# Two graph-attention layers on one core: the first output projection tile by tile with the normalization in it, and a head end in two parts

## The reference

```python
x1 = relu(x @ W_ah + b_ah)
xs = [relu(gat_conv(x1, src, dst, W, a_s, a_d, b)) for W, a_s, a_d, b in three]   # 4 heads of 192 each
y  = relu(concatenate(xs, axis=1) @ W_out + b_out)        # [1250, 2304] @ [2304, 768]
x2 = layernorm(x + y)
h  = elu(gat_layer(x2, W1 [768, 2048], 4 heads of 512) + b1)
z  = gat_layer(h, W2 [2048, 768], 1 head) + b2
return layernorm(x2 + z)
```

## Time and profile before

| | us |
|---|---|
| median of 3 runs | 2097.6 (2096.47 to 2100.13) |
| the profiled execution | 2099.49 |
| its span (first to last instruction) | 2097.7 |
| PE busy | 1865.0 (89%) |
| DVE busy | 1492.5 (71%) |
| ACT busy | 974.5 (46%) |

### The profile page before, as it was taken

How to read it: one execution, slowest core, us unless ns; L and a number is a source line. 1 busy time by engine, 2 the same in 40 slices (tenths; PEclk the granted TensorE clock), 3 DMA queues, 4 the chain that set the end, 5 groups by cost and what they waited for, 6 DMA issues and landing times. The chain is left out here.

```text
span 2097.7 us, 29944 instructions
## 1 busy us (share of the span) xinstructions
PE 1865.0 (89%) x11272; PEld 1774.4 (85%) x11272; DVE 1492.5 (71%) x2490; ACT 974.5 (46%) x1463; POOL 166.1 (8%) x139
## 2 busy tenths in 40 slices
PE   5998899994999999994989889979999996999888
PEld 4666689994999999994989779978999995999888
DVE  7887759996888888862556619717888885235776
ACT  1222222215687897763222322217888885232433
POOL 5010022100000000000001012100000000000210
PEclk9999999996999999996999889989999998999999
DMA  3111154335243424307856445544423404644402
GB/s 115 49 53 49 38 157 147 104 87 137 65 130 95 108 87 123 89 13 219 236 138 184 137 149 151 169 129 131 143 82 106 139 34 132 176 108 131 116 1 74
DMA packets 203354, 237.69 MB, mean 113 GB/s; under 512 B 98741, under 2 KB 177677, under 8 KB 203224
## 3 DMA queue, kind: packets, MB, share of 16 engines
q1 hardware_dynamic: 195240, 208.32, 34.5%
q0 software_dynamic: 7216, 24.91, 4.0%
q10 hardware_dynamic: 768, 2.70, 0.4%
HBM read 173.99 MB, written 61.90 MB: 112 GB/s over the span
## 5 line engine op out<-in xcount | busy, mean ns | idle before, releaser
L946 PE MATMUL p_o<-h_in,p 125*125 125x193 f32 x2400 | 405.5, 332 | 41.5 <-DVE p L905 20.9
L946 PEld LDWEIGHTS p_o<-h_in,p 125*125 125x125 f32 x2400 | 399.3, 191 | 44.8 <-issue 23.7
L866 ACT ACTIVATE e<-uv,col 125x1250 f32<-125x1250 f32 x240 | 298.5, 1358 | 16.0 <-DMA uv<-uv_rows 14.9
L1404 PE MATMUL p_o<-p_hi,h_parts 125*128 125x416 f32 (+1 forms) x960 | 282.8, 355 | 24.7 <-DVE p_lo L1338 18.4
L1686 PE MATMUL p_y<-fw_hi,f_hi 128*125 128x384 f32 (+1 forms) x680 | 237.9, 350 | 60.7 <-DVE f_lo L1562 58.6
L1686 PE MATMUL p_y<-fw_lo,f_hi 128*125 128x384 f32 (+1 forms) x680 | 235.3, 346 | 0.0
L1686 PE MATMUL p_y<-fw_hi,f_lo 128*125 128x384 f32 (+1 forms) x680 | 234.6, 345 | 0.0
L1562 DVE TENSOR_TENSOR f_lo<-f_raw,f_hi 128x1125 fp32r<-128x1125 f32 (+1 forms) x80 | 101.1, 1265 | 173.6 <-ACT f_hi L1660 173.5
L900 DVE TENSOR_TENSOR e<-e 125x1250 f32<-125x1250 f32 x120 | 174.1, 1451 | 67.5 <-ACT e L866 67.4
L1404 PEld LDWEIGHTS p_o<-p_hi,h_parts 125*128 125x128 f32 x960 | 181.7, 189 | 30.8 <-issue 18.6
L1660 ACT ACTIVATE f_hi<-f_raw 128x1125 fp32r<-128x1125 f32 (+1 forms) x80 | 87.4, 1093 | 251.3 <-PE p_y L1686 215.3
(11 more groups left out here) (227 smaller groups left out, 3259.4 us busy)
## 6 DMA issues: line engine op xcount, KB each, us to landing
f_raw<-turned SPq DMA_DIRECT2D x40, 562.5 KB, 4.3
f_raw<-turned SPq DMA_DIRECT2D x40, 500.0 KB
h_rows<-h_out SPq DMA_DIRECT2D x32, 560.0 KB
h_parts<-h_rows SPq DMA_DIRECT2D x40, 448.0 KB
uv<-uv_rows SPq DMA_DIRECT2D x24, 546.9 KB
turned<-out_f SPq DMA_DIRECT2D x18, 625.0 KB
h_rows<-h_out SPq DMA_DIRECT2D x24, 424.4 KB
h_in<-h_rows SPq DMA_DIRECT2D x24, 424.4 KB
```

The costliest lines, as they stand in the source:

```text
L866: last = a.activation(e[:, g % RING, kind, :], uv[:, hh, kind, :], ACT.Exp, bias=col_src[kind][:, bass.ds(i * 2 + hh, 1), s])
L946: last = nc.tensor.matmul(p_o[:, b, n * 256:n * 256 + C0 + 1], p[:, g % RING, d * T:(d + 1) * T], h_in[:, hh, s, 0:C0 + 1], start=(s == 0 ...
L1404: last = nc.tensor.matmul(p_o[:, bank(n, c), 0:w], h[:, s, kind, cols].bitcast(F32R), pp[:, g % RING, 0:w], start=(s == 0 and j == 0), sto ...
```

## The change

1. `aggregate_layer0`: `divisors` works in two parts. The first takes the sums of tiles 0 to 3 (banks 0 and 1) as soon as PE has finished tile 3 in the head's last step (`banks_done`), the second those of tiles 4 to 9 at the step's end. ACT waits for the first part ahead of tile 0 and for the second ahead of tile 4. DVE stands one step earlier for it (after g = 11 and g = 1 in place of 12 and 2).
2. `turned0` is laid out `[NT, 128, KO, T]`: a store writes runs of 500 bytes, and a piece of a tile is read in runs of 4,500 bytes.
3. `G` is stored to memory (3.1 MB) behind the loads of the second iteration. After the last load of the stage, its place takes the first five of 18 blocks of `w_out`, all 768 columns each, and the first piece of tile 0.
4. `project_out_layer0` takes the place of `from_turned` and `normalize`: all of `w_out` stays on chip as two roundings, the tiles are done once, both halves of the columns in two PSUM banks, and each tile is normalized when it is summed, with tiny instructions of one column, and stored to `x2_rows`. `x` is loaded into three slots.
5. `project_layer1` loads the rows of `x2` in four slots, turns five tiles ahead of the first product and the other five between the first tiles, adds `b2` on DVE and stores the sum to `base_rows`; the scores come after tile 9, the mask is loaded back, and the maxima begin at tile 18.
6. `aggregate_last` loads `base_rows`; POOL's additions are gone.

```diff
@@ aggregate_layer0
             load(0)
             load(1)
+            dma_in_two(sp, core.mask_rows, core.G.rearrange("p t n -> p (t n)"), mask_saved)
...
+            for k in range(W_AHEAD):
+                sp.dma_start(w_ahead[:, k, :], w_out[:, k * 128:(k + 1) * 128, :].rearrange("h p c -> p h c")).then_inc(ahead_in, 16)
+            sp.dma_start(f_ahead[:, 0], turned_rows[0, :, 0:KO // 2, :]).then_inc(ahead_in, 16)
             store(ITERS - 2)
             store(ITERS - 1)
...
+                        if s == NT - 1 and d == 2 * FIRST - 1:
+                            last.then_inc(banks_done, 1)
@@ project_out_layer0 (new), DVE
+            for t in range(1, NT):
+                rest_of_f(t, 0)
+                for n in range(weighed.chunks * (t - 1) // (NT - 1), weighed.chunks * t // (NT - 1)):
+                    weighed.reduce(dve, n, ...)
+                rest_of_f(t, 1)
+                leave(t - 1)
+            leave(NT - 1)
@@ project_layer1, SP
+            load_x(0)
+            load_w(0)
+            dma_in_two(sp, b_row[:], bias.rearrange("(o f) -> o f", o=1).broadcast_to([T, D]), bias_in)
+            for t in range(1, XR):
+                load_x(t)
+            load_w(1)
+            for t in range(XR, NT):
+                store_base(t - XR)
+                load_x(t)
@@ aggregate_last
-        @block.gpsimd
-        def _(pool):
-            pool.wait_ge(base_in, 64)
-            for t in range(NT):
-                pool.tensor_tensor(y2[:, t, :], y2[:, t, :], b_row[:], ALU.add).then_inc(base_done, 1)
```

More of the change, by code:

```diff
@@ L887, in divisors @@
             def divisors(i, hh):
[L888 to L893, removed]
+                for n, (b0, b1) in enumerate(((0, FIRST), (FIRST, BANKS))):
+                    if n == 0:
+                        dve.wait_ge(banks_done, i * 2 + hh + 1)
+                    else:
+                        dve.wait_ge(p_used, i * STEPS + ((hh + 1) * NT + 2 * NT))
+                    v.tensor_scalar(sums[:, 0, 2 * b0:2 * b1].rearrange("p (b n) -> p b n", n=2),
+                                    p_o[:, b0:b1, :].rearrange("p b (n c) -> p b n c", n=2)[:, :, :, C0],
+                                    1e-16, None, ALU.add).then_inc(sum_steps, 1)
+                    dve.wait_ge(sum_steps, (i * 2 + hh) * 4 + 2 * n + 1)
+                    v.reciprocal(sums[:, 1, 2 * b0:2 * b1], sums[:, 0, 2 * b0:2 * b1]).then_inc(sum_steps, 1)
             def body(i, first):
@@ L986, in project_layer1 @@
         p_h = pb("p_h", [T, 4, 512])
-        p_r = pb("p_r", [R, 3, 512])
+        p_r = pb("p_r", [128, 3, 512])
         p_s = pb("p_s", [128, 512])
+        bias_in = sem("bias_in")
+        mask_in = sem("mask_in")
+        x_loaded = [sem(f"x2_loaded{r}") for r in range(XR)]
+        x_turned = sem("x2_turned")
+        x_rounded = sem("x2_rounded")
+        x_split = sem("x2_split")
+        base_done = sem("base_done")
+        base_stored = [sem(f"base_stored{r}") for r in range(XR)]
         w_in = [sem(f"pw_in{u}") for u in range(2)]
@@ L1038, in _ @@
                 sp.wait_ge(h_stored[part], 64 * UNITS)
+            for r in range(XR):
+                sp.wait_ge(base_stored[r], 32 * len(range(r, NT, XR)))
             sp.wait_ge(uv_stored, 32)
@@ L1077, in _ @@
                     act.wait_ge(uv_turned, 1)
[L1078 removed]
+                    a.activation(turned_uv[:], p_s[0:heads * NT, 0:2 * T].rearrange("p (a q) -> p a q", a=2), ACT.Copy).then_inc(uv_kept, 1)
                     act.wait_ge(uv_kept, 1)
@@ L1112, in spread @@
                 v.scalar_tensor_tensor(v_col[:, 0:heads, :], score[:, 1], SLOPE, tmp2[:], ALU.mult, ALU.subtract).then_inc(max_steps, 1)
+            for t in range(TURNED_FIRST):
+                rest_of_x(t)
             for n in range(TILES):
                 q, t = divmod(n, NT)
+                if n + TURNED_FIRST < NT:
+                    rest_of_x(n + TURNED_FIRST)
+                if n == NT:
+                    keep_scores()
                 dve.wait_ge(h_rounded, n + 1)
@@ L1148, in _ @@
                 last.then_inc(h_summed, 1)
+                if n + TURNED_FIRST < NT:
+                    turn_x(n + TURNED_FIRST)
+                if n == NT - 1:
+                    scores()
+                    turn_scores()
                 if n == UV_AT + 4:
@@ L1796, in aggregate_last @@
-def aggregate_last(nc, core, h2, uv, col_src, bias, x2_dram, y2, out):
+def aggregate_last(nc, core, h2, uv, col_src, base_rows, y2, out):
     CT = core.CT
```

432 lines of the change are left out of this document (293 added, 139 removed).

## The result

The changed kernel takes 2063.27 us (median of 4 runs, 2061.53 to 2063.97), the kernel before 2098.86 beside it (2096.47 to 2100.46): a ratio of 0.9832, 95% interval 0.9815 to 0.9848. The gain is 35.6 us; 46.6 was forecast (2097.6 to 2051). The profiled execution's span is 2061.2 us against 2097.7, 36.5 less. Cut at landmarks that both traces have, these 36.5 lie as follows.

A forecast was written before the change was run, and what follows sets the result against it. PE, 89% busy, was taken to bound the kernel, so its idle time was counted: -16.5 - 0.2 - 29.5 + 5.8 - 5.9 = -46.3 us against the median 2097.6 gave 2051. Its own range was 2042 to 2060, the wider one 2036 to 2069.

The forecast's parts named there:

- rival 1: After the projection, x2's round trips set PE's pace: cycle of 6 us, first product at 22, 2068 us; 15 in 100.
- Heads, -16.5: Ends of heads in the first aggregation: of 20.7 us of PE's idle time some 4 stay; bounds -20.7 and -11.
- The last head's stores, +1.1: End of the first aggregation: stores in 500-byte runs cost +1.1 us, from 0 to +4; with fewer copies, -0.2 together.
- the rate of reads of 500-byte runs: Last head's stores: 6.50 MB read in some 20 us, 325 GB/s, so 0.64 MB of stores take 2.0 us.
- The doubling that it noted: Last head's stores: by the skill's 512-byte rule the last store takes about twice as long, the sum some 2 us more.
- Projection, 196.8: First projection, load to last sum: tile 0 in 28.4 us, tiles 1 to 9 in 168.4; against 226.3, -29.5.
- The wait for the last blocks: Tile 0 of the projection: 21.6 us of loads, the first landing after 2.5; last block there at 24.5 us.
- 0.1733 a product: Projection: PE's time per product, 61.00 / 352 us; 108 products make 18.7 us a tile.
- Behind it, +5.8: From the projection's last sum to the rounding of tile 79: 220.2 us against 214.4, from 0 to +18.
- the round trip: Layer after the projection: SP's cycle of store, wait and load, 2.7 + 0.75 = 3.45 us; each of six maybe 2 longer.
- The price of the lower clock: Start of the layer after the projection: the lower clock costs 2.6 us, given as 0.26 x 12.
- Last stage, -5.9: Last stage without POOL's additions: PE's gap of 4.23 us and 1.7 of half clock go; from -3 to -9.

The follow-up runs named there:

- the place alone: The kernel before with DVE taking the head's sums one step earlier, but all ten tiles at once; median 2084.5 us, ratio 0.9941.
- the split alone: The kernel before with the head's sums in two parts, but DVE's old place for them; median 2092.09 us, ratio 0.9969.

## Why the prediction was right, and where it was off

- **Direction and range held,** by the mechanisms that it named: heads, one pass over the weights, POOL out of the last stage, given back in part behind the projection. The forecast's own range, 2042 to 2060, did not hold: 2063.27 lies above it, toward rival 1. That it missed by no more is in part luck, since the heads gained 6.3 us for a reason that it left out.
- **Heads, -16.5, measured -22.8.** Mis-sized. The idle time left was right (4.3 us). The step took only idle time and left out the lower clock behind three of the gaps, 1.7 us each, though the same account was made for the last stage. It also treated the place as a side matter of the split; alone the split is worth 2.6.
- **The last head's stores, +1.1, measured +2.8 to +4.8.** Mis-sized, and beyond its bound of 4 in the profiled run. The step took the rate of reads of 500-byte runs for the price of such writes. That row is a weak one even for reads: half its packets are short, but at 500 bytes each they are 1.4 of its 6.50 MB. The doubling that it noted beside it was the better guide: 1.6 us of moving became 4.2. Against it stands the shorter head end, -2.5 in place of -1.3, again by the clock.
- **Projection, 196.8, measured 200.7.** The first product (3.5 us in) and the seam behind it (9.5 against 10) were right. Tile 0 ends 29.9 us in, not 28.4: while the ring is full, the loads don't run. The wait for the last blocks was also summed 0.4 too long (21.6 + 2.5 is 24.1, not 24.5). Tiles 1 to 9 take 170.8, not 168.4. Half of that is a misreading: 0.1733 a product came from a count of 352 in 61 us that takes in products cut by the window's ends, where the pieces of 54 products stand 9.42 us apart in the kernel before, 0.1744 each. The other half is the changed kernel's own: its pieces stand 9.48 us apart, 0.1756, and no run shows why.
- **Behind it, +5.8, measured +13.7.** The step that failed is the round trip. Rival 1 had its first product right (at 22 us; measured 21.6), and its cycle of 6 us too long. The prediction priced the store by the kernel's last one, which runs alone (2.7 us). Here the first store runs behind 3.5 MB of loads, and the load that waits for it is issued 6.3 us after it; in the steady cycle SP spends 4.3 to 4.8 us, since it issues nothing while it waits. The waits cost the first product 2.4 to 2.7 us (28.7 and 28.4 without them, against 31.1) and the tiles behind it 7.2 to 8.1 (189.0 to 189.8 us, against 197.1). The price of the lower clock was also summed wrong, 0.26 x 12 being 3.1 and not 2.6; it decides nothing.
- **Last stage, -5.9, measured -4.7.** Right. Putting the additions back costs 5.4. But the size is loose: from the stage's first product to the end, the seven kernels without POOL's additions take 125.6 to 127.4 us, the five with them 127.4 to 133.9.

What stays open: 19.3 us of the projection's gain are idle time of PE and 6.2 are faster products, but apart from the blocks ahead no run takes its parts (one pass of weights, no drained pieces, normalization in it) one by one.

## What to carry to other kernels

Price a gap with the clock behind it. A wait at the end of a short phase costs by where its releasing engine stands in its own order, so try its place as well as its length: here the place alone gave 10.9 us, the split alone 2.6, and both 22.8. When a stage starts from memory, sort its loads by whether they depend on the stage before: those that don't are best issued in that stage, and a queue that waits for a landing should first issue whatever else is ready.

## What the runs showed of the hardware

- A store of 0.64 MB in runs of 500 bytes moved in 3.0 to 4.2 us, at up to 290 GB/s at first and at 120 to 160 later; in runs of 5,000 it moved in 1.6 us at some 400. Reads in runs of 500 passed at the rate of longer ones (5.70 against 5.73 MB in a stage's first 21.5 us).
- The lower clock followed idle gaps of PE of 2.56 us and more at the ends of heads, seven times out of eight in two runs (the kernel before and the split alone), and no gap of 1.45 us or less; each time it cost some 1.7 us of work (a mean clock of 0.79 over 8 us).
- DVE's addition of two SBUF tensors took 2.93 us in the layer after, beside POOL's split, and 0.95 otherwise:

```profile
1166.84 2.93 DVE L1172 TENSOR_TENSOR x_in<-x_in,b_row 125x768 f32<-125x768 f32 x1
```

```profile
1165.49 3.46 POOL L1102 TENSOR_TENSOR pw_lo<-pw_raw,pw_hi 128x1536 fp32r<-128x1536 f32 x1 [47.59 <-ACT pw_hi L1112]
```

  The Trainium skill, "GPSIMD Engine Reference", section "Specifications", says that POOL and VectorE contend for SBUF when an instruction reads two SBUF inputs; the trace agrees, here and in the earlier trace rows. But 3 is no fixed factor. The addition ends at 1169.77 us, 0.82 behind the end of POOL's split (1168.95), and in the last stage of the kernel before DVE's ten operations beside POOL's ten additions take 2.29 to 2.61 us, and each ends 0.67 to 0.82 us behind the end of one of these. That is how it looks if such an operation stands until POOL's instruction is through and only then takes its own time; its price is then what is left of POOL's instruction.
- The price of such contention is not the same each time: with the same additions on POOL, the last stage's products took 118.3 us where POOL began 18.8 us behind the first of them (the run with the place alone), and 121.2 to 124.8 in four runs where it began 13.0 to 16.8 us behind. Without the additions they took 116.5 to 118.3. Whether its start decides stays open, as no run moves it alone.
